# Wider table rows and smaller gather chunks in the second graph of a two-graph transformer layer

## The reference

```python
edge_index = stack([src, dst])                      # first graph: 200,000 edges, 12,500 nodes
xn = layernorm(x)                                   # x: 12500 x 256
x = x + gnn(xn, edge_index, ...) + mix(xn, ...)     # graph convolution + linear attention
xf = layernorm(x)
# ffn: a graph attention router over the second graph (131,072 edges + 12,500 loops) ...
h = (xf @ W_gat).reshape(M, 4, 4)                   # HEADS=4, EXPERTS=4
a_src, a_dst = (h * att_src).sum(-1), (h * att_dst).sum(-1)
e = leaky_relu(a_src[src] + a_dst[dst], 0.2)
ee = exp(e - segment_max(e, dst)[dst])
alpha = ee / segment_sum(ee, dst)[dst]
agg = segment_sum(h[src] * alpha[:, :, None], dst)  # scores: layernorm, mean over heads, top 2, softmax
# ... and four experts over every node, weighted with the router's gates g
for ei in range(4):
    out = out + g[ei] * (gelu(xf @ W1[ei] + b1[ei]) @ W2[ei] + b2[ei])
```

## Time and profile before

| | us |
|---|---|
| median of 3 runs | 6403.15 (6402.35 to 6422.75) |
| the profiled execution, its own time | 6419.1 |
| its span, first to last instruction | 6417.1 |
| TensorE busy in it | 4381.1 |
| VectorE busy | 2724.0 |
| GpSimd busy | 2976.3 |
| ScalarE busy | 759.1 |
| mean granted TensorE clock | 0.748 of full speed |

### The profile page before, as it was taken

One profiled execution on the slowest core, in us unless ns is written; L12 is line 12 of the kernel. 1 busy time (PEld: TensorE's weight loads), 2 busy tenths in 40 slices (PEclk: granted clock), 3 DMA queues, 4 the chain that ended last, 5 costly groups with the idle time before them and its releaser, 6 DMA issues. The chain is left out here.

```text
span 6417.1 us, 45813 instructions
## 1 busy us (share of the span) xinstructions
PE 4381.1 (68%) x14757; PEld 2842.7 (44%) x14757; DVE 2724.0 (42%) x5225; ACT 759.1 (12%) x1439; POOL 2976.3 (46%) x2919
## 2 busy tenths in 40 slices
PE   6998777788688887787755324954954774773067
PEld 4776544444455555555545112632622442441045
DVE  6786566565555456666555000211211211221255
ACT  1113311222100000000001000110210110110022
POOL 0000467667656557777720774146146326334500
PEclk8667988889878877777765556966966886885588
DMA  2112433333345543333465211211211211221168
GB/s 70 52 52 56 142 111 116 112 111 118 107 128 150 138 126 97 89 89 90 87 123 154 53 9 25 68 25 35 68 25 35 52 41 35 51 44 28 23 158 218
DMA packets 241828, 531.23 MB, mean 83 GB/s; under 512 B 73332, under 2 KB 147415, under 8 KB 234822
## 3 DMA queue, kind: packets, MB, share of 16 engines
q1 hardware_dynamic: 121909, 293.42, 16.8%
q0 software_dynamic: 119696, 235.05, 15.7%
HBM read 377.97 MB, written 150.28 MB: 82 GB/s over the span
## 5 line engine op out<-in xcount | busy, mean ns | idle before, releaser
L933 POOL DMA_INDIRECT g_rows<-table,gcn_srcT x1664 | 1780.5, 1070 | 778.3 <-issue 477.9
L1794 POOL DMA_INDIRECT n_rows<-gtab,so_own x1122 | 1082.8, 965 | 1255.0 <-DVEq L1911 913.8
L1742 PE MATMUL p_py<-f_w,f_hh 128*125 128x256 f32 x2688 | 723.1, 407 | 778.6 <-issue 778.6
L1003 PE MATMUL g_ps<-g_rows,g_hot 128*125 128x256 f32 x3328 | 1085.9, 465 | 224.9 <-issue 151.9
L1288 DVE TENSOR_TENSOR acc<-acc,g_ps 125x256 f32 x1664 | 697.5, 419 | 908.8 <-PE g_ps L1003 463.7
L1742 PEld LDWEIGHTS p_py<-f_w,f_hh 128*125 128x125 f32 x2688 | 539.3, 201 | 984.0 <-issue 921.6
L1935 DVE TENSOR_TENSOR p_ob<-p_py,p_xb 125x512 f32<-125x512 f32 x168 | 114.6, 691 | 1982.2 <-remote 924.4
L1003 PEld LDWEIGHTS g_ps<-g_rows,g_hot 128*125 128x125 f32 x3328 | 711.5, 229 | 505.9 <-issue 340.9
L1736 PE MATMUL p_ph<-f_xfT,f_w 128*128 128x500 f32 x1344 | 656.2, 630 | 279.6 <-issue 211.1
L1736 PEld LDWEIGHTS p_ph<-f_xfT,f_w 128*128 128x128 f32 x1344 | 271.5, 202 | 625.5 <-issue 620.3
L1964 ACT ACTIVATE f_hh<-p_ph,f_b 128x500 f32<-128x500 f32 x336 | 224.8, 677 | 1965.8 <-remote 1142.2
(11 more groups left out here) (329 smaller groups left out, 4119.9 us busy)
## 6 DMA issues: line engine op xcount, KB each, us to landing
o_d<-p_ob SPq DMA_DIRECT2D x21, 1920.0 KB
z_ob<-o_d SPq DMA_DIRECT2D x21, 1920.0 KB
g_rows<-table,gcn_srcT POOLq DMA_INDIRECT x1664
n_rows<-gtab,so_own POOLq DMA_INDIRECT x1122
gout<-n_o SPq DMA_DIRECT2D x11, 1224.0 KB
xnT_d<-a_xnT SPq DMA_DIRECT2D x25, 500.0 KB, 2.9
m_area<-xnT_d SPq DMA_DIRECT2D x25, 500.0 KB
qT_d<-m_area SPq DMA_DIRECT2D x25, 500.0 KB
```

Of the source, the lines that this page charges most:

```text
L933: pool.indirect_dma_start(out=rows[:, g % RING, j], out_offset=None, in_=K.table, in_offset=bass.IndirectOffsetOnAxis(ap=K.gcn_srcT[:, 4 * ...
L1003: mm = pe.matmul(ps[q, p % 4, b], hot[:, g % 4, 2 * j + b], rows[:, g % RING, 2 * j + b], start=True, stop=True, skip_group_check=True)
L1742: mm = pe.matmul(py[0:TN, e % 2, j // 2, (j % 2) * D:(j % 2 + 1) * D], self.hh[:, e % 2, c, j * TN:(j + 1) * TN], self.w2[:, e, c], start= ...
L1794: pool.indirect_dma_start(out=rows[:, c % 3, j], out_offset=None, in_=K.gtab, in_offset=bass.IndirectOffsetOnAxis(ap=K.gat_src[:, c * W + ...
```

## The change

- A row of `gtab` becomes `TWIDE` = 128 floats (512 bytes) long; the first 24 hold what they held. The other 104 floats of each row are written once with zeros, from a tile `a_blank`, by one DMA at the head of `first_half`. The store of the 24 floats at the end of `second_norm` now goes into rows with a pitch of 512 bytes.
- Every gather now brings 512 bytes per row. `n_rows` holds three slots of 34 columns of 512 bytes (before: three of 102 columns of 96 bytes).
- A chunk is 34 columns, so there are 33 of them. Each has the same 37 steps on DVE and ACT on a third of the columns, and one store.
- Chunks are dealt with between units: `at_unit` = 4, 7, 10, 13, ..., one chunk for every 3.1 units; `to_exponents` after the unit, ACT's exponential and `sums` after the next. 26 chunks lie between units, 7 after the last unit. The first three chunks are gathered without a wait, as before.

```diff
+TWIDE = 128
@@ first_half, sync
                 load(1)
                 load(2)
+                sp.wait_ge(blank_s, 1)
+                sp.dma_start(K.gtab.rearrange("(t p) f -> p t f", p=TN)[:, :, TROW:TWIDE],
+                             blank[q].unsqueeze(1).to_broadcast([TN, NT, TWIDE - TROW])).then_inc(blank_s, 16)
                 for k in range(NB):
...
+                sp.wait_ge(blank_s, 17)
@@ second_norm, sync
-                sp.dma_start(K.gtab.rearrange("(t p) f -> p t f", p=TN), trow[0:TN]).then_inc(S["out"], 16)
+                sp.dma_start(K.gtab.rearrange("(t p) f -> p t f", p=TN)[:, :, 0:TROW], trow[0:TN]).then_inc(S["out"], 16)
@@ gat_experts
-    W = 102
+    W = 34
     chunks = GC // W
-    at_block = [3, 5, 8, 10, 12, 15, 17, 19]
+    units = EARLY * NE
+    at_unit = [4 + 31 * c // 10 for c in range(chunks) if 5 + 31 * c // 10 < units]
...
-        rows = m.sb("n_rows", [P, 3, W, TROW])
+        rows = m.sb("n_rows", [P, 3, W, TWIDE])
@@ gat_experts, vector
-                for k in range(EARLY):
-                    for e in range(NE):
-                        take(k, e)
-                        if k in at_block and e == 0:
-                            to_exponents(at_block.index(k))
-                        if k in at_block and e == 2:
-                            sums(at_block.index(k))
-                for c in range(len(at_block), chunks):
+                for u in range(units):
+                    take(*divmod(u, NE))
+                    if u - 1 in at_unit:
+                        sums(at_unit.index(u - 1))
+                    if u in at_unit:
+                        to_exponents(at_unit.index(u))
+                for c in range(len(at_unit), chunks):
@@ program
-        K.gtab = m.dram("gtab", [N, TROW])
+        K.gtab = m.dram("gtab", [N, TWIDE])
```

More of the change, by code:

```diff
@@ L417, in first_half @@
         deg = m.sb("a_deg", [P, NT])
+        blank = m.sb("a_blank", [P, TWIDE - TROW])
         pdeg = m.ps("a_pdeg", [P, 2, P])
@@ L423, in first_half @@
         (w_s, both_s, numbered, node_s, tile_s, used, st_s, mv_s, eps_s, root_s, rec_s, xn_s, turned, xnT_s, h_s, hT_s,
-         stat_s, deg_s, v) = (m.sem("a_" + s) for s in (
+         stat_s, deg_s, v, blank_s) = (m.sem("a_" + s) for s in (
              "w", "both", "numbered", "node", "tile", "used", "st", "mv", "eps", "root", "rec", "xn", "turned", "xnT",
-             "h", "hT", "stat", "deg", "v"))
+             "h", "hT", "stat", "deg", "v", "blank"))
         x_in = [m.sem(f"a_x_in{s}") for s in range(3)]
@@ L1757, in gat_experts @@
         X = K.expert
-        rows = m.sb("n_rows", [P, 3, W, TROW])
-        first = m.sb("n_first", [P, TROW])
+        rows = m.sb("n_rows", [P, 3, W, TWIDE])
+        first = m.sb("n_first", [P, TWIDE])
         zero = m.sb("n_zero", [P, TROW])
@@ L1825, in _ @@
                 sp.dma_start(K.gout[LIST:LIST + P], zero[:]).then_inc(zeroed, 16)
-                for k in range(EARLY):
[L1827 to L1832, removed]
-                for c in range(len(at_block), chunks):
+                for u in range(units):
+                    if u - 1 in at_unit:
+                        keep(at_unit.index(u - 1))
+                    k, e = divmod(u, NE)
+                    if e == NE - 1:
+                        if k + 2 < EARLY:
+                            load(k + 2)
+                        sp.wait_ge(ob_s, (k + 1) * OBS)
+                        rows_in_two(sp, K.o_d[k], ob[:, k % 2], kept[k % 2])
+                for c in range(len(at_unit), chunks):
                     keep(c)
@@ L1974, in _ @@
                 act.wait_ge(w_s, 64 * NE)
[L1975 to L1980, removed]
+                for u in range(units):
+                    gelu(*divmod(u, NE))
+                    if u - 1 in at_unit:
+                        chunk(at_unit.index(u - 1))
+                for c in range(len(at_unit), chunks):
                     chunk(c)
```

1 line of the change is left out of this document (added).

## The result

| | before | after |
|---|---|---|
| median, us | 6412.95 (6402.35 to 6455.88) | 6004.23 (5965.19 to 6014.81) |
| span of the profiled execution | 6417.1 | 6013.1 |
| `gat_experts`: its first gather to `gat_finish` | 3538.4 to 5977.3, 2438.8 | 3562.6 to 5574.9, 2012.2 |
| TensorE busy, mean clock | 4381.1, 0.748 | 4326.3, 0.772 |

The account below looks back on a forecast made before the run. TensorE, slowed by long rows of gathers, was taken to bound `gat_experts`. Profile time 6419.1 - 1004 (slowdown gone) + 15 (zeros) = 5430, with the median 16 below: 5414 us; range 5375 to 6040.

Parts of the forecast that it names:

- the hold: In `gat_experts`, some 26 us into a row of gathers, TensorE issues one weight-load/matmul pair per 2.80 us, not 0.28.
- The step that failed: In `gat_experts`, 512-byte gathers would act like the first graph's 1,024-byte ones, so TensorE's slow issue goes; chance 0.46.
- The gain of 1004 us: `gat_experts`: with TensorE unhindered, GpSimd's 1,122 gathers decide and `gat_finish` starts at 4972.9 instead of 5977.3.
- The premise below it: First graph's gathers of 1,024-byte rows, at a pitch of 1.36 to 1.43 us, never slow TensorE's issue.
- the third case: Rival in `gat_experts`: row size does not matter, small chunks lose 19 us each; gain 460, 5958 us; chance 0.18.
- the tail: Behind the last gather of `gat_experts`: landing 2.4 us, last chunk on VectorE 9.5, then 5.9 + 0.6 to the next phase.
- GpSimd's path, had there been no hold: `gat_experts`: 1,122 gathers at 1.261 us without a wait, from 3539.7 to 4954.5, decide the phase's length.
- Zeros: Head of `first_half`: one DMA of 12,500 pieces of 416 bytes, 36 to 88 us, makes block 3 late; +15 us.
- The 140 us worked out beside the rule: Zeros in `first_half`: if 125 partitions use only 5 engines, the store takes some 140 us and costs 65, not 15.
- Chunk work: VectorE in `gat_experts`: 33 chunks of 9.5 us, 314 against 217, hidden under TensorE and POOL; costs nothing.
- ScalarE's table: `gat_experts`: ACT changes its table twice for 26 chunks instead of eight, inside TensorE's 13.6 us per unit; costs nothing.
- SP's `keep`: `gat_experts`: SP waits for `sums` ahead of a block's load that is due a whole block (54 us) later; costs nothing.

Follow-up runs that it names:

- e4: Kernel before (96-byte rows, 102-column chunks) with a memset behind each gather, pitch 1.55 us; chip 5: 5848 us, 0.912 of the kernel before.
- e12: Changed kernel with 96-byte rows, no zeros, memset behind gathers of the first 24 chunks (pitch 1.42), one chunk per 3.6 units; chip 10: 5625 us, 0.883 of before.
- e16: Kernel before, unchanged, a single profiled run on chip 13: 5266 us.
- e1: Changed kernel with table rows back at 96 bytes and no store of zeros; chip 5: 5962 us, 0.926 of the kernel before.
- e11: Changed kernel with 96-byte rows, no zeros, 1-column memset behind each gather (pitch 1.33), one chunk per 3.3 units; chip 5: 5871 us, 0.913 of before.
- e13: Changed kernel with 96-byte rows, no zeros, memset behind gathers of the first 25 chunks (pitch 1.37), one chunk per 3.5 units; chip 10: 5780 us, 0.908 of before.
- e17: Changed kernel, unchanged, on chip 13: 5223 us, 0.993 of the kernel before.
- e2: Changed kernel with 96-byte rows, no zeros, memset behind each gather (pitch 1.55), one chunk per 3.8 units; chip 5: 5788 us, 0.901 of before.

## Why the prediction was wrong

- *What bounds the kernel.* Right: TensorE, by the hold; where e4 and e12 took the hold away, the time went. But the prediction took it for a property of the kernel. On chips 13 and 15 the same kernel has none, and is 1,153 us shorter (span 5263.9 in e16): 923 of it in this phase, 229 ahead of it.
- *The step that failed* is "I take it that 512-byte rows behave like the 1,024-byte rows, and the hold goes". The gain of 1004 us that was put on it needed the 778.6 us of "issue" gone; 261.9 stayed, and the phase gained 426.6. What the runs show in its place: at a pitch of 1.25 rows of 512 and of 96 bytes are held alike (the changed kernel, and e1), and with rows of 96 bytes throughout the hold is there at 1.33 and 1.37 us (e11, e13) and gone at 1.42 (e12) and 1.55 (e4). It is the pitch, and the size plays no part in the hold. The doubt was on the page (the 1,024-byte gathers at 1.36 to 1.43 us) and got too little weight.
- *The premise below it* is false too: "TensorE is never held there", in the stage of the 1,024-byte gathers. All of the 229 us lie in that stage. Its gathers, in the profile of before and in e16, the same kernel on chip 13:

```profile
L933 POOL DMA_INDIRECT g_rows<-table,gcn_srcT x1664: 940/946/3173, 697.1 to 3254.8; - x185
L933 POOL DMA_INDIRECT g_rows<-table,gcn_srcT x1664: 941/949/2466, 696.8 to 3026.8; - x185
```

  That is 2557.7 us against 2330.0; in all runs on chips 5 and 10 it is 2518 to 2584, in all on 13 and 15 2325 to 2339. In the profile of before TensorE starts no matmul for more than 4 us 33 times there, 221 us together; in e16 four times, 20 us. All runs on chips 5 and 10 have 27 to 37 such stops (170 to 247 us), all on 13 and 15 four to seven (20 to 33 us). They look like the second shape: TensorE's last matmul for it is out at 1188.4, ScalarE goes on at 1196.3 and TensorE, behind VectorE, at 1199.9 (TensorE, then ScalarE):

```profile
1188.40 0.69 PE L1025 MATMUL m_pb<-m_area,ones 1*125 1x256 f32 x2
...
1199.89 3.38 PE L1023 MATMUL m_pb<-m_area 128*125 128x512 f32 x4 [8.88 <-DVE m_area L1298]
```

```profile
1196.26 0.38 ACT L1188 ACTIVATE m_area<-m_pb 125x256 f32<-125x256 f32 x1 [4.61 <-remote]
```

  So big rows did not leave TensorE alone. The earlier trace rows are from windows in which it happens to be seldom. No experiment changed the pitch in this stage.
- *The rival that happened* was the third case: the hold does not see the size, and small chunks dodge part of it. Its 19 us lost per chunk were 17, its 5958 was 6004; it had a chance of 0.18. The agreement is in part luck: the row of the first 306 gathers, the full stops and the tail were not sized one by one. What it lacks is 9 us at the start (24.2 instead of 15) and 17 in the tail, the rest lies in between. The last gather starts at 5539.83 and `gat_finish` 35 us later, where 18.4 was summed; on chip 13 it is 16.6. In its last chunk VectorE is held as well, with idle times such as these, which chip 13 does not have; the second waits only for VectorE's own instruction before it, which started at 5550.99, 2.80 us (twice 1.40) earlier:

```profile
5550.28 0.17 DVE L1897 COPY n_mx<-n_mx 128x4 f32<-128x4 f32 x1 [9.52 <-remote]
...
5553.79 0.83 DVE L1902 TENSOR_TENSOR_SCAN n_ad<-so_x,n_ad,n_am 128x34 f32<-128x34 f32 x4 [2.41 <-remote]
```

- *GpSimd's path, had there been no hold*, was well sized: 1,433 us for the phase were forecast, 1,454 are measured on chip 13 (1.281 us per gather instead of 1.261).
- *Zeros.* The store was put at 36 to 88 us, at 416 bytes about 57, and its cost at +15. It took 54 (the load behind it stood 54.5), and what follows came 18 us later (17.7 on chip 13: 714.5 instead of 696.8 for the first gather of the first graph). Both were well sized. But the prediction set aside the rule of the Trainium skill's "DMA: Bandwidth & Descriptors", section on why a DMA increments its semaphore by 16, which gives 5 engines for 125 partitions, because the store of 96-byte pieces "was busy like 8 engines". The trace agrees with the rule, for both stores: their semaphores get their last five steps at 107.9 to 109.3 us (zeros) and at 3535.6 to 3535.7 (the store of `gtab` in the kernel before), where a store from 128 partitions (`xnT_d`, near 59.3 us in the kernel before) gets sixteen. The share of busy time adds up packets that overlap on one engine (105% in the earlier trace rows), so it does not count engines. The 140 us worked out beside the rule rested on a price of 56 ns per piece, that of 800 bytes; five engines at the 54 us measured are 22 ns per piece on each.
- *Chunk work, ScalarE's table, SP's `keep`:* hidden, as forecast. TensorE waited 128.5 us for `f_hh`, but 110 of these are the five full stops, and in e12 1.6 are left.

**The pitch as an explanation, and what stays open.** Most of what chips 5 and 10 show fits one picture: something takes one gather per 1.40 us, gathers issued faster pile up by the difference, and once some 3.6 us are piled up TensorE gets one instruction per gather taken. It gives the onset at 1.25 us (24 gathers, measured 18 to 33), that there is none at 1.42, the end behind the last gather (n x 0.15 - 3.6 = 11.7 us for 102, measured 11.0 to 16.9; 1.5 for 34, measured 1.6 to 4.5) and GpSimd's own 1.40 us after 186 gathers. It does not give the onset at the pitches between: 50 gathers at 1.33, measured 22 to 50, ten of thirteen at 32 or below; 120 at 1.37, where TensorE's first gap comes after 38 and the steady hold after 46 to 62. So a fixed pile of 3.6 us is not what sets the hold off. It is an argument from numbers: no run shows what it is that piles up. The transfers do not fill the DMA engines, whose share is 11.3% in the hold; that TensorE's program comes late is not seen either, since no block of instructions is fetched in that window. VectorE is held too, so it need not be a thing of TensorE. One rival was not tested: every time here is of an execution that the profiler recorded, and no run tells whether the hold is there without its records. Nor is it known what differs between the chips.

## To carry to other kernels

A difference between two stages of one trace (here 1,024-byte rows, taken to be without the hold, and 96-byte rows with it) is evidence for a cause only when nothing else differs; look for the second difference and give it its share of the chance. An experiment that changes the suspected rate alone (a memset of known length behind each gather) is cheap and decides it. And a large loss with the releaser "issue" should be looked at on a second chip before a kernel is shaped around it: here pacing gains 12% on one kind of chip and costs 2% on the other. That second chip also shows what the first one's trace hides: the stage that was taken for free of the loss was 229 us longer by it.

## What was not expected of the hardware

- TensorE held to one instruction per 1.40 us beside gathers of 128 rows that GpSimd issues every 1.25 us (to one or two at 1.33 and 1.37), with no engine, DMA queue or wait of the profile to show for it; gone at 1.42 (e12) and 1.55 (e2, e4). VectorE shows it in the tail, and the stage of the 1,024-byte gathers has stops of 4 to 17 us.
- It appears on two of four chips, and there every time: the kernel before takes 6345 to 6452 us on chips 5 and 10 and 5245 to 5279 on 13 and 15. Single gathers are stretched on both kinds of chip (up to 1.97 us in the profile of before, 1.94 and more in e16).
- Gathers of 512-byte rows are no slower to issue than those of 96 bytes: 0.977 us each in e17, 1.021 in e16.
